# Layer norm by packed variances on column and row tiles, tap sums moved into the first blur, last blur rows added by VectorE

## The chip, the cores and the metric

One NeuronCore of a Trainium2 chip. The metric is the device time of one execution in microseconds (us), as the median of several runs. The kernel before takes 470.53 us (median of 3 runs, 469.13 to 471.44).

## What is computed

The input x has 8 images of 16 channels of 64 x 64 pixels in float32. Four layers follow each other:

- L0: a layer norm over the 16 channels at every pixel, three depthwise convolutions along the rows and three along the columns, a projection, and attention along rows and columns with 8 heads.
- L1 and L3: a blur with 9 x 9 weights that depend on the pixel, added to x, and then an instance norm over the 4096 pixels of each of the 128 planes.
- L2: 3 x 3 convolutions with binarised weights, batch norm, a residual and a clip.

The part of the reference around the change, cut to what matters:

```
# L0, at each pixel of an image
mean, var over the 16 channels;  x = (x - mean) / sqrt(var + 1e-5) * ln_w + ln_b
# L1, L3
enhanced = x + low_freq                      # low_freq: the blurred x
out = (enhanced - mean) / sqrt(var + 1e-5)   # over the 4096 pixels of a plane
# L2: out1 = conv(x + shift1, sign(w)), out2 = conv(x + shift2, sign(w)), out = out1 + w1 * out2
```

## The kernel before, in words

The 128 partitions hold 8 images times 16 channels, and the free axis the 4096 pixels, in 8 chunks of 512 (one bank of PSUM, the tile `ps`, each). Each layer is one or more blocks; a block gives every engine its own list of instructions, semaphores order them by hand, and the next block begins when all engines have ended their lists. There are only a few loops in the program (the middle heads of the attention); all else is written out.

**`l0_norm` (L145 to L359)** is the first block. SyncE's queue loads `centre` and x in four parts (L201), then stores the summed taps to DRAM (`band`, L204), waits for that and loads them back shifted (`windows`, L212), then loads the tables that later layers need (L214). ScalarE's queue loads nine small constants (L299, L302) and ScalarE waits for all of them (L303). TensorE multiplies each chunk by `centre` (x minus its mean, L240), VectorE copies the result to `xc` (L336), ScalarE squares it (L306). Variances come from eight matmuls with `meansel` (L251), each on a tile of 32 columns of the array, into two banks; they are copied out (L340, L309), turned by transposes (L259), get eps added (L345), then a square root (L311) and a reciprocal over 256 elements (L348). The 256 values per partition are widened to 4096 by eight copies on VectorE and eight on ScalarE (`widen`, L294), and 32 transposes turn them back (L268). VectorE scales each chunk (L354), ScalarE applies weight and bias (L318), and TensorE turns the chunks into `xrow` and `xcol` (L282), which VectorE and ScalarE copy out in turns (L359, L324). GpSimd meanwhile clears `pad_a` and builds `toep` with two large products (L224, L228) from `windows`. The next block, `l0_conv`, begins with matmuls on `toep` (L430).

**`blur` (L882 to L1267)** runs twice, for L1 (tag g1) and L3 (tag g3), over 8 rows of blocks r. TensorE computes logits on row tiles (L1065), ScalarE takes exp (L1074), TensorE sums (L1088) on column tiles, VectorE swings, normalises and turns the sums (L1098, L1106, L1113), and GpSimd adds them to the padded image (`pool_enhance`, L1118); VectorE takes statistics of that row (`dve_stats`, L1123). After the last row come the mean, the variance and `norm` (L1254 to L1259). In the first blur VectorE also makes the binary weights `wb` (L1273, L1275).

**`binconv` (L1279 to L1446)** normalises 8 groups of 8 rows (VectorE, L1370), rounds them to `high` (ScalarE, L1362), takes `rest` as the difference (VectorE, L1375), and convolves both parts with nine taps, 18 matmuls per group (TensorE, L1346). Behind the first group TensorE computes the tap sums, nine matmuls with two columns (L1354), into bank 7; VectorE waits for them (L1398), makes a map of them (to L1424), and then goes through the groups (L1425 on).

Of the kernel before, what the change touches and what calls it, by code (L numbers as in the profile page):

```python
# [23 lines left out]
F32 = mybir.dt.float32  # L24
# [38 lines left out]
        "g1_b1", "g1_b2", "g3_b1", "g3_b2"]  # L63
# [8 lines left out]
def build(nc, d, band, out):  # L72

    keep = ExitStack()
    with keep:
# [50 lines left out]
        with ExitStack() as g:  # L126
            negative = sb(g, "negative", [P, TAPS * P])
            raw, raw_in = later["c_weight"]
            wb_ready = sem("wb_ready")
            blur(nc, sem, lambda n, s: sb(g, "g1_" + n, s), "g1", later, ident, vec, ps, pad_a, norm, pad_b, None, None,  # L130
                 beside=lambda dve: binary_weights(dve, raw, negative, wb, raw_in, wb_ready))
        with ExitStack() as c:
            binconv(nc, sem, lambda n, s: sb(c, n, s),
                    lambda n, s: c.enter_context(nc.sbuf_tensor(n, s, F32R)), vec, ps, wb, norm, pad_a, pad_b)
# [10 lines left out]
def l0_norm(nc, sem, sb, d, ident, vec, pad_a, ps, x0, xrow, xcol, toep, onehot, beta,  # L145
            projblk, const_in, later, band, x_again):


    centre = sb("centre", [P, P])
    meansel = sb("meansel", [P, 32])  # L150
    var_row = sb("var_row", [P, 2 * BANK])
# [8 lines left out]
    var = sb("var", [P, PXT * B])  # L160
    std = sb("std", [P, PXT * B])
    rstd = sb("rstd", [P, PXT, B])
    wide = sb("wide", [P, PXT, CP, B, HEADS])

    x_in = [sem(f"x_in{j}") for j in range(4)]
    centre_in = sem("centre_in")
    centred = sem("centred")
# [11 lines left out]
    var_out = [sem(f"var_out{a}") for a in range(2)]  # L179
    var_turned = sem("var_turned")  # L180
    eps_added = sem("eps_added")
    rooted = sem("rooted")
    rstd_ready = sem("rstd_ready")
    rstd_wide = [sem(f"rstd_wide{cp}") for cp in range(CP)]
# [6 lines left out]
    CONSTS = 8  # L191

    with nc.Block() as block:
        @block.sync
        def _(sp):
# [38 lines left out]
        def _(pe):  # L234
            pe.wait_ge(centre_in, 16)

            for j in range(CHUNKS):
# [4 lines left out]
            pe.wait_ge(const_in, 16 * CONSTS)  # L242
            pe.wait_ge(xc_copied, 5)

            pe.matmul(ps[:, 4, 0:2], bias_rhs[:], bias_lhs[:], start=True, stop=True).then_inc(bias_mm, 1)

            for a in range(2):
                pe.wait_ge(xc_copied, 6 + a)
                for q in range(4):
                    pe.wait_ge(squared, 4 * a + q + 1)  # L250
                    mm = pe.matmul(ps[32 * q:32 * q + 32, 5 + a, :], meansel[:],  # L251
                                   sq[:, BANK * (4 * a + q):BANK * (4 * a + q + 1)], start=True, stop=True)
                mm.then_inc(var_mm, 1)

            for a in range(2):
                pe.wait_ge(xc_copied, 1 + a)
                pe.wait_ge(var_out[a], 1)
                for c in range(4):
                    tr = pe.transpose(ps[:, a, P * c:P * c + P], var_row[:, BANK * a + P * c:BANK * a + P * c + P],  # L259
                                      ident[:])  # L260
                tr.then_inc(var_turned, 1)

            pe.wait_ge(bias_read, 1)
            for t in range(PXT):
                if t % 4 == 0:
                    for cp in range(CP):
                        pe.wait_ge(rstd_wide[cp], t // 4 + 1)
                tr = pe.transpose(ps[:, t // 4, P * (t % 4):P * (t % 4) + P],  # L268
                                  wide[:, t].rearrange("p c b n -> p (c b n)"), ident[:])
                if t % 4 == 3:  # L270
                    tr.then_inc(rstd_spread, 1)

            for base, lines in ((0, sq[:].rearrange("p (i m) -> p i m", m=P)),
# [17 lines left out]
        def widen(copy, j, cp):  # L291

            tiles = slice(4 * j, 4 * j + 4)
            copy(wide[:, tiles, cp], spread(rstd[:, tiles, :].unsqueeze(3), [P, 4, B, HEADS]))\  # L294
                .then_inc(rstd_wide[cp], 1)

        @block.scalar
        def _(act):
            act.dma_start(taps[:], d["taps"]).then_inc(taps_in, 16)  # L299
            for t, name in ((meansel, "meansel"), (ident, "ident"), (vec, "vec"), (bias_lhs, "bias_lhs"),  # L300
                            (bias_rhs, "bias_rhs"), (onehot, "onehot"), (mask, "mask"), (projblk, "projblk")):
                act.dma_start(t[:], d[name]).then_inc(const_in, 16)  # L302
            act.wait_ge(const_in, 16 * CONSTS)  # L303
            for j in range(CHUNKS):
# [3 lines left out]
            act.wait_ge(var_mm, 2)  # L308
            act.copy(var_row[:, BANK:2 * BANK], ps[:, 6, :]).then_inc(var_out[1], 1)  # L309
            act.wait_ge(eps_added, 2)  # L310
            act.activation(std[:], var[:], ACT.Sqrt).then_inc(rooted, 1)  # L311
            act.wait_ge(rstd_ready, 1)
            for j in range(CHUNKS):
                widen(act.copy, j, 1)

            for j in range(CHUNKS):
# [1235 lines left out]
```

## Time and profile before

| | |
|---|---|
| median of 3 runs | 470.53 us |
| the profiled execution | 471.36 us |
| span of its trace, first to last instruction | 469.4 us |
| TensorE matmuls busy | 394.1 us (84%) |
| VectorE busy | 276.3 us (59%) |
| ScalarE busy | 241.5 us (51%) |
| GpSimd busy | 108.2 us (23%) |

In the rows below PE is TensorE (PEld its weight loads), DVE VectorE, ACT ScalarE, POOL GpSimd, SP SyncE; L336 is line 336 of the kernel before. A float32 matmul stands as two records (passes) in the trace; a transpose or an fp32r matmul as one. Times of the timeline are microseconds from the start of the span; spans on POOL are rough.

### The profile page before, as it was taken

The page shows a single profiled execution, that of the slowest core. Times are in us where ns is not written, and L with a number is a line of the kernel's source. Part 1 is how long each engine was busy: PE and PEld are TensorE (multiplying, and loading weights), DVE is VectorE, ACT ScalarE, POOL GpSimd, SP SyncE. Part 2 cuts the span into 40 slices and gives each one's busy share as a digit, 9 for nine tenths or more (in the row PEclk, how much of TensorE's full clock was granted, in tenths as well). Part 3 has the DMA queues.
Part 4 walks back from the last instruction along what each step waited for, and adds up shares of the span by engine and source line. Part 5 has one row for each costly group of instructions (what it writes and reads, how often), then busy time and mean ns, then how long its engine had stood idle before and what let it go on. Part 6 is the DMA issues. An engine that isn't in the chain of part 4 may idle for free. (4 is left out here: it accounts for less than half of the span.)

```text
span 469.4 us, 15959 instructions
## 1 busy us (share of the span) xinstructions
PE 394.1 (84%) x7136; PEld 245.7 (52%) x7136; DVE 276.3 (59%) x459; ACT 241.5 (51%) x310; POOL 108.2 (23%) x134
## 2 busy tenths in 40 slices
PE   4758998887499999988899999939998889999980
PEld 1247882322289885134555555528773555555550
DVE  1697369576378889747744353465845654343453
ACT  1548258566543331143478888810103538888772
POOL 3050002122200000075027223110007513224211
PEclk9959999898999999989999999969999999999995
DMA  8860000000000000000000000000000000000004
GB/s 182 166 257 1 1 1 1 0 1 0 1 3 3 1 3 1 1 1 1 1 4 4 4 3 5 4 1 0 1 0 2 1 1 4 4 4 3 4 4 179
DMA packets 8239, 10.14 MB, mean 22 GB/s; under 512 B 5535, under 2 KB 6896, under 8 KB 8048
## 3 DMA queue, kind: packets, MB, share of 16 engines
q1 hardware_dynamic: 7152, 8.82, 6.8%
q8 instruction: 54, 0.88, 0.8%
q10 hardware_dynamic: 1024, 0.36, 0.4%
q14 instruction: 9, 0.07, 0.1%
HBM read 7.06 MB, written 2.11 MB: 20 GB/s over the span
## 5 line engine op out<-in xcount | busy, mean ns | idle before, releaser
L1074 ACT ACTIVATE g_wgt<-ps 128x1024 f32<-128x1024 f32 x128 | 124.1, 1021 | 39.6 <-PE ps L1065 39.6
L1088 PEld LDWEIGHTS ps<-g_wgt,g_xt 128*17 128x17 f32 x4096 | 58.8, 97 | 47.7 <-ACT g_wgt L1074 43.1
L1065 PE MATMUL ps<-g_diag,g_exponents 32*128 32x512 f32 x512 | 73.7, 638 | 9.0 <-ACT g_wgt L1074 5.2
L1088 PE MATMUL ps<-g_wgt,g_xt 128*17 128x64 f32 x4096 | 69.9, 220 | 2.6 <-DVE g_xt L1051 1.9
L1098 DVE STREAM_TRANSPOSE g_swung<-ps 128x512 f32<-128x512 f32 x32 | 23.0, 717 | 80.1 <-PE ps L1088 80.1
L1130 POOL TENSOR_TENSOR g_diag<-g_scl,hot 128x512 f32<-128x512 f32 x32 | 33.3, 1059 | 32.1 <-PE ps L1065 25.4
L1346 PE MATMUL ps<-high,wb 128*128 128x512 f32 x72 | 30.4, 423 | 8.1 <-DVE rest L1375 8.1
L470 PE MATMUL ps<-conv_img,projblk 128*32 128x512 f32 x256 | 35.5, 689 | 0.0
L527 ACT ACTIVATE biased<-ps,beta_o 128x512 f32<-128x512 f32 x32 | 24.7, 799 | 15.7 <-PE ps L470 15.7
L1065 PEld LDWEIGHTS ps<-g_diag,g_exponents 32*128 32x128 f32 x512 | 21.4, 182 | 19.2 <-ACT g_wgt L1074 8.1
L1346 PE MATMUL ps<-rest,wb 128*128 128x512 f32 x72 | 30.1, 418 | 0.0
L974 ACT ACTIVATE g_hid<-ps,vec 128x512 f32<-128x512 f32 x16 | 11.0, 688 | 33.8 <-PE ps L961 33.8
L667 ACT ACTIVATE e<-ps 128x512 f32<-128x512 f32 x16 | 9.6, 597 | 31.7 <-PE ps L629 31.7
L1051 DVE COPY g_xt<-ps 128x512 f32<-128x512 f32 x30 | 19.5, 683 | 8.8 <-PE ps L1045 8.8
L470 PEld LDWEIGHTS ps<-conv_img,projblk 128*32 128x32 f32 x256 | 13.0, 118 | 21.6 <-issue 17.5
L1045 PE MATMUL ps<-ident,g_wgt 128*128 128x128 f32 x144 | 20.5, 281 | 4.4 <-DVE g_xt L1051 3.8
L1118 POOL TENSOR_TENSOR pad_b<-pad_b,g_low 128x512 f32<-128x512 f32 x8 | 10.2, 1269 | 51.2 <-DVE g_low L1113 51.2
L1045 PEld LDWEIGHTS ps<-ident,g_wgt 128*128 128x128 f32 x144 | 15.2, 140 | 12.4 <-issue 8.8
L1029 POOL COPY g_wgt<-pad_b 128x512 f32<-128x512 f32 x18 | 10.3, 626 | 46.6 <-POOLq L1335 45.0
L1118 POOL TENSOR_TENSOR pad_a<-pad_a,g_low 128x512 f32<-128x512 f32 x8 | 10.1, 1269 | 46.5 <-DVE g_low L1113 46.5
L1346 PEld LDWEIGHTS ps<-high,wb 128*128 128x128 f32 x72 | 14.5, 202 | 12.1 <-DVE rest L1375 8.3
L618 PE MATMUL ps<-ident,rnh 128*128 128x128 f32 x128 | 18.8, 295 | 2.3 <-POOL rnh L710 2.3
(164 smaller groups left out, 640.0 us busy)
## 6 DMA issues: line engine op xcount, KB each, us to landing
x<-in_x SPq DMA_DIRECT2D x8, 256.0 KB, 7.0
x<-in_x SPq DMA_DIRECT2D x1, 2048.0 KB, 8.7
out<-pad_a SPq DMA_DIRECT2D x4, 512.0 KB, 3.9
windows<-band SPq DMA_DIRECT2D x4, 256.0 KB, 5.1
c_weight<-in_c_weight SPq DMA_DIRECT2D x1, 576.0 KB, 4.3
g_gband<-in_g_gband SPq DMA_DIRECT2D x2, 128.0 KB, 2.9
g_w<-in_g_w SPq DMA_DIRECT2D x2, 128.0 KB, 2.7
onehot<-in_onehot ACTq DMA_DIRECT2D x1, 128.0 KB
```

The lines of the kernel that those rows point to most:

```text
L470: mm = pe.matmul(ps[q:q + 32, j % 4, :], projblk[:, 64 * cp + 32 * late:64 * cp + 32 * late + 32], lines(t, inner, strip, side), start=Tru ...
L527: act.activation(biased[:, j % 4, :], ps[:, j % 4, :], ACT.Identity, bias=beta[:, t:t + 1], scale=1.0).then_inc(proj_biased, 1)
L618: tr = pe.transpose(ps[:, NORM[t % 2], P * k:P * k + P], spread(rnh[s][:, 4 * t + k:4 * t + k + 1], [P, P]), ident[:])
L1045: tr = pe.transpose(ps[:, XT_BANK[k], P * j:P * j + P], tile(g)[:, cb].rearrange("p r c -> p (r c)"), ident[:])
L1051: copy(xt[g][:, 4 * k:4 * k + 4, :, 0:C], ps[:, XT_BANK[k], :].rearrange("p (k b m) -> p k b m", k=4, b=B)).then_inc(done, 1)
L1065: mm = pe.matmul(ps[:, pair(2 * f + g // 2) + g % 2, :], gband[part, t, :], diag[r % 2][h][part].rearrange("p a n -> p (a n)"), start=True ...
L1074: act.activation(wgt[r % 2][h][:, t, parity].rearrange("p u a n -> p (u a n)"), ps[:, pair(n):pair(n) + 2, :].rearrange("p u n -> p (u n)" ...
L1088: mm = pe.matmul(ps[32 * j:32 * j + MX, O_BANK[h], 64 * cb:64 * cb + 64], xt[r + t][:, cb, 2 * j + h, :], wgt[r % 2][h][:, t, parity, :, 4 ...
L1098: dve.transpose(swung[h][:].rearrange("p a n -> p (a n)"), ps[:, O_BANK[h], :]).then_inc(swung_out, 1)
L1118: pool.tensor_tensor(rows, rows, low[r % 2][:].rearrange("p (k r c) -> p r k c", k=CB, r=BLK), ALU.add)\
L1130: pool.tensor_tensor(diag[r % 2][h][:], spread(own.unsqueeze(2), [P, 16, 32]), spread(hot[:].unsqueeze(1), [P, 16, 32]), ALU.mult).then_in ...
L1346: mm = pe.matmul(ps[:, g % 4, :], wb[:, t, :], part[:, ROWS * g + dh:ROWS * g + dh + ROWS, dw:dw + W], start=(k == 0), stop=(k == 2 * TAPS ...
```

## The change

It has four parts. In `l0_norm`, the variances of four chunks are packed into one 128 x 128 piece by 16 matmuls with N = 128 on four column tiles, ScalarE takes the square root of it directly from PSUM (eps as its bias, after a first square root of one column that only brings the table), VectorE inverts it, and 16 matmuls on four row tiles spread it over the four chunks' banks; this is done for each half of the chunks, the first half ahead of the last two centring matmuls. The loads change places: ScalarE's queue loads the taps, `meansel` (now 64 KB) and `vec`, stores `band`, and loads three more; SyncE's queue takes `spreadsel` (new, 64 KB), `ident`, `onehot` and `projblk`, the last two behind `windows`. In the blurs, the last row is added by VectorE in place of GpSimd. The tap sums are computed at the end of TensorE's list in the first blur, into bank 4. And the first group of the convolutions takes its nine `high` taps as soon as `high` is there, and then the nine `rest` taps.

```diff
@@ l0_norm, @block.sync
-            sp.wait_ge(taps_summed, 2)
-            sp.dma_start(band, taps[:, 0, :]).then_inc(band_out, 16)
+            sp.dma_start(spreadsel[:], d["spreadsel"]).then_inc(spreadsel_in, 16)
+            sp.dma_start(ident[:], d["ident"]).then_inc(tables_in, 16)
             sp.wait_ge(band_out, 16)
...
+            for t, name in ((onehot, "onehot"), (projblk, "projblk")):
+                sp.dma_start(t[:], d[name]).then_inc(tables_in, 16)
             for name, (t, arrived) in later.items():
@@ l0_norm, @block.tensor
+            def variances(a):
+                pe.wait_ge(xc_copied, PART * (a + 1))
+                pe.wait_ge(squared, PART * (a + 1))
+                for v in range(PART):
+                    for u in range(PART):
+                        first = BANK * (PART * a + u) + P * v
+                        mm = pe.matmul(ps[32 * u:32 * u + 32, PART * a, 0:P], meansel[:, v, :],
+                                       sq[:, first:first + P], start=(v == 0), stop=(v == PART - 1))
+                mm.then_inc(var_mm, 1)
+            def spread_out(a):
+                pe.wait_ge(rstd_ready, a + 1)
+                for v in range(PART):
+                    for u in range(PART):
+                        part = slice(32 * u, 32 * u + 32)
+                        mm = pe.matmul(ps[:, PART * a + u, P * v:P * v + P], spreadsel[part, v, :],
+                                       rstd[part, a, :], start=True, stop=True)
+                mm.then_inc(rstd_spread, 1)
+            for j in range(6):
+                centre_of(j)
+            pe.wait_ge(first_in, 16 * FIRST)
+            variances(0)
+            for j in range(6, CHUNKS):
+                centre_of(j)
...
+            pe.wait_ge(spreadsel_in, 16)
+            spread_out(0)
+            variances(1)
+            pe.wait_ge(bias_read, 1)
+            spread_out(1)
+            pe.wait_ge(tables_in, 16 * TABLES)
@@ l0_norm, @block.scalar
+            for t, name in ((meansel, "meansel"), (vec, "vec")):
+                act.dma_start(t[:], d[name]).then_inc(first_in, 16)
+            act.wait_ge(taps_summed, 2)
+            act.dma_start(band, taps[:, 0, :]).then_inc(band_out, 16)
+            for t, name in ((bias_lhs, "bias_lhs"), (bias_rhs, "bias_rhs"), (mask, "mask")):
                 act.dma_start(t[:], d[name]).then_inc(const_in, 16)
+            act.wait_ge(first_in, 16 * FIRST)
+            act.activation(root_first[:], vec[:, VEC["ln_eps"]:VEC["ln_eps"] + 1], ACT.Sqrt)
+            for j in range(6):
+                square(j)
+            root(0)
+            for j in range(6, CHUNKS):
+                square(j)
+            root(1)
@@ l0_norm, @block.vector
+            for j in range(6):
+                copy_out(j)
+            inverse(0)
+            for j in range(6, CHUNKS):
+                copy_out(j)
...
+            for j in range(2):
+                scale(j)
+            inverse(1)
+            for j in range(2, CHUNKS):
+                scale(j)
@@ blur
-                pool_enhance(pool, r)
+                if r + 1 < RB:
+                    enhance(pool, r)
...
+            if after_sums is not None:
+                after_sums(pe)
...
+            enhance(dve, RB - 1)
             dve_stats(dve, RB - 1)
+TAP_BANK = 4
+def tap_sums(pe, ps, wb, vec, ready, done):
+    pe.wait_ge(ready, 2)
+    for t in range(TAPS):
+        mm = pe.matmul(ps[:, TAP_BANK, 2 * t:2 * t + 2], wb[:, t, :].bitcast(F32), ...)
+    mm.then_inc(done, 1)
@@ binconv, @block.tensor
+            pe.wait_ge(rounded, 1)
+            for t in range(TAPS):
+                tap(0, t, high, t == 0, False)
+            pe.wait_ge(split, 1)
+            for t in range(TAPS):
+                mm = tap(0, t, rest, False, t == TAPS - 1)
...
-                if g == 0:
-                    for t in range(TAPS):
-                        mm = pe.matmul(ps[:, TAP_BANK, 2 * t:2 * t + 2], wb[:, t, :].bitcast(F32), ...)
-                    mm.then_inc(tap_mm, 1)
```

## Rows read from the trace of the kernel before

**Rows 1.** Timeline of the first 46 us: start, length (us), engine, line, [idle before <-releaser].

```profile
14.05 4.26 ACT L306 ACTIVATE sq<-xc 128x512 f32<-128x512 f32 x8 [3.05 <-DMA projblk<-in_projblk]
14.42 0.69 DVE L336 COPY xc<-ps 128x512 f32<-128x512 f32 x1 [0.17 <-PE ps L240]
...
14.75 1.98 PE L240 MATMUL ps<-x,centre 128*128 128x512 f32 x4 [0.37 <-DMA x<-in_x]
...
21.80 1.75 DVE L348 RECIPROCAL rstd<-std 128x256 f32<-128x256 f32 x1 [0.66 <-ACT std L311]
...
22.86 3.60 POOL L224 TENSOR_TENSOR toep<-windows,mask 128x2048 f32<-128x2048 f32 x1 [17.71 <-DMA windows<-band]
...
23.59 7.84 DVE L294 COPY wide<-rstd 128x256 f32<-128x256 f32 x8
...
26.42 3.65 POOL L228 TENSOR_TENSOR toep<-windows,mask 128x2048 f32<-128x2048 f32 x1
...
31.35 2.47 DVE L354 TENSOR_TENSOR xc<-xc,ps 128x512 f32<-128x512 f32 x4
32.06 5.76 ACT L318 ACTIVATE sq<-xc,vec 128x512 f32<-128x512 f32 x8 [5.93 <-DVE xc L354]
...
45.13 8.83 PE L430 MATMUL ps<-xrow,toep 128*128 128x256 f32 x32 [2.19 <-PEq L193]
```

**Rows 2.** Line L294 alone: durations in ns, minimum/median/maximum, first and last start.

```profile
L294 DVE COPY wide<-rstd x8: 279/280/3683, 23.6 to 31.1; 128x256 f32<-128x256 f32 x8
```

**Rows 3.** Groups by line: busy us, mean ns of one, idle before.

```profile
L1435 DVE TENSOR_TENSOR resid<-pad_a,shift_map 128x512 f32<-128x512 f32 x8 | 5.5, 685 | 0.0
...
L558 DVE RECIPROCAL rn<-root 128x128 f32<-128x128 f32 x1 | 1.0, 953 | 0.4 <-ACT root L535 0.4
...
L535 ACT ACTIVATE root<-nsq 128x128 f32<-128x128 f32 x1 | 0.3, 309 | 3.4 <-DVE nsq L556 3.4
```

**Rows 4.** Timeline of TensorE in three later stretches, columns as in rows 1.

```profile
298.06 1.14 PE L1065 MATMUL ps<-g_diag,g_exponents 32*128 32x512 f32 x8 [0.22 <-ACT g_wgt L1074]
299.13 1.09 PE L1088 MATMUL ps<-g_wgt,g_xt 128*17 128x64 f32 x64
...
319.85 2.06 PE L1354 MATMUL ps<-vec,wb 128*128 128x2 f32 x18
321.78 0.49 PE L1346 MATMUL ps<-high,wb 128*128 128x512 f32 x1
...
356.00 0.65 PE L990 MATMUL ps<-g_hid,g_w 128*32 128x128 f32 x16 [0.18 <-DVE g_hid L981]
```

**Rows 5.** Timeline from the first blur's last row to the first convolution.

```profile
306.59 0.71 DVE L1113 STREAM_TRANSPOSE g_low<-g_mix 128x512 f32<-128x512 f32 x1
307.38 1.26 POOL L1118 TENSOR_TENSOR pad_a<-pad_a,g_low 128x512 f32<-128x512 f32 x1 [5.91 <-DVE g_low L1113]
308.67 0.69 DVE L1123 BATCH_NORM_STATS2 g_stats<-pad_a 128x6 f32<-128x512 f32 x1 [1.37 <-POOL pad_a L1118]
...
312.27 0.85 DVE L1375 TENSOR_TENSOR rest<-pad_a,high 128x660 fp32r<-128x660 f32 x1 [0.38 <-ACT high L1362]
...
313.18 0.79 PE L1346 MATMUL ps<-high,wb 128*128 128x512 f32 x1 [8.14 <-DVE rest L1375]
```

**Rows 6.** Line L1118, both blurs: who waited for it (us in total, times).

```profile
  DVE g_stats L1123: 2.7, 2
```

**Rows 7.** Stretches: length, busy us (instructions) of PE, PEld, DVE, ACT, POOL; granted clock; DMA.

```profile
46.00:48.00 2.00, 2.00 (x6) 1.64 (x5) 0.69 (x1) 0.00 (x0) 0.00 (x0) 0.50 0.01 4
49.00:52.00 3.00, 3.00 (x15) 2.64 (x15) 1.28 (x2) 0.94 (x2) 0.00 (x0) 1.00 0.00 0
...
313.20:318.00 4.80, 4.80 (x11) 3.77 (x12) 1.61 (x7) 0.65 (x1) 0.00 (x0) 0.50 0.00 0
...
322.00:340.00 18.00, 18.00 (x77) 14.20 (x77) 16.26 (x42) 3.28 (x5) 0.00 (x0) 1.00 0.00 1
```

**Rows 8.** DMA issues: KB each, us to landing.

```profile
band<-taps SPq DMA_DIRECT2D x1, 15.9 KB, 8.7
```

More of the change, by code:

```diff
@@ L234, in _, with centre_of @@
         def _(pe):
-            pe.wait_ge(centre_in, 16)
-            for j in range(CHUNKS):
+            def centre_of(j):
                 if j % 2 == 0:
@@ L299, in _, with square @@
             act.dma_start(taps[:], d["taps"]).then_inc(taps_in, 16)
-            for t, name in ((meansel, "meansel"), (ident, "ident"), (vec, "vec"), (bias_lhs, "bias_lhs"),
-                            (bias_rhs, "bias_rhs"), (onehot, "onehot"), (mask, "mask"), (projblk, "projblk")):
+            for t, name in ((meansel, "meansel"), (vec, "vec")):
[3 more added lines that the diff above has]
+            for t, name in ((bias_lhs, "bias_lhs"), (bias_rhs, "bias_rhs"), (mask, "mask")):
                 act.dma_start(t[:], d[name]).then_inc(const_in, 16)
-            act.wait_ge(const_in, 16 * CONSTS)
-            for j in range(CHUNKS):
+            def square(j):
                 act.wait_ge(xc_copied, j + 1)
@@ L307, in _, with root @@
                                ACT.Square).then_inc(squared, 1)
[L308 to L314, printed above, removed]
+            def root(a):
+                act.wait_ge(var_mm, a + 1)
+                act.activation(std[:, a], ps[:, PART * a, 0:P], ACT.Sqrt,
+                               bias=vec[:, VEC["ln_eps"]:VEC["ln_eps"] + 1], scale=1.0).then_inc(rooted, 1)
+            act.wait_ge(first_in, 16 * FIRST)
[6 more added lines that the diff above has]
+            root(1)
             for j in range(CHUNKS):
@@ L879, in l0_out, with blur @@
     return on_tensor, on_scalar, on_vector
-def blur(nc, sem_, sb, tag, later, ident, vec, ps, pad, norm, to_clear, result, out, beside=None):
+def blur(nc, sem_, sb, tag, later, ident, vec, ps, pad, norm, to_clear, result, out, beside=None, after_sums=None):
     def sem(name):
@@ L1337, in _, with tap @@
         def _(pe):
-            for g in range(CHUNKS):
+            def tap(g, t, part, first, last):
+                dh, dw = t // 3, t % 3
+                return pe.matmul(ps[:, g % 4, :], wb[:, t, :],
+                                 part[:, ROWS * g + dh:ROWS * g + dh + ROWS, dw:dw + W], start=first, stop=last)
+            pe.wait_ge(rounded, 1)
[4 more added lines that the diff above has]
+                mm = tap(0, t, rest, False, t == TAPS - 1)
+            mm.then_inc(conv_mm, 1)
+            for g in range(1, CHUNKS):
                 pe.wait_ge(split, g + 1)
@@ L1341, in _ @@
                     pe.wait_ge(lin_ready, g - 3)
[L1342 removed]
                 for t in range(TAPS):
[L1344 to L1356 removed]
+                    tap(g, t, high, t == 0, False)
+                    mm = tap(g, t, rest, False, t == TAPS - 1)
+                mm.then_inc(conv_mm, 1)
         @block.scalar
@@ L1473, in shape_constants @@
     onehot = np.tile(np.eye(8, 32, dtype=np.float32), (P, 1, 1))
-    return {"ident": ident, "centre": centre, "meansel": meansel,
+    return {"ident": ident, "centre": centre, "meansel": meansel, "spreadsel": spreadsel,
             "onehot": onehot, "mask": mask, "gmask": gmask, "hot": hot}, (u, v, inside)
```

112 lines of the change are left out of this document (37 added, 75 removed).

## The prediction

> **What bounds the kernel now.** I read the timeline first, stage by stage, because a share over the whole span says nothing of the three places that change. In each place the question is which wait ends last.
>
> *Layer norm.* The block runs one chain [rows 1]. ScalarE's squares don't begin until 14.05: they wait for `projblk`, the last of nine constants, though VectorE is by then about to copy chunk 5 (14.42 + 0.69 = 15.11). The inverse root is there at 23.55 (21.80 + 1.75). Then comes the dearest piece: eight widening copies hold VectorE for 7.84 us, to 31.43. They are not long of themselves. The shortest and the median take 0.28 us, the longest 3.68 [rows 2]; in 23.59 to 30.1 GpSimd runs its two `toep` products of 3.60 and 3.65 us [rows 1], and the longest copy is about as long as one of them. Scaling follows (pitch 2.47 / 4 = 0.62 us), then weight and bias on ScalarE (pitch 5.76 / 8 = 0.72), which end at 37.82, and the turning up to the next block's first matmul at 45.13.
>
> *End of each blur.* VectorE's turned row is ready at 307.30; GpSimd adds it, and VectorE's statistics begin at 308.67 after an idle 1.37 us [rows 5]. It occurs twice, 2.7 us in all [rows 6].
>
> *Convolutions.* TensorE starts at 313.18 because `rest` ends at 313.12 (312.27 + 0.85); `high` was there at 312.27 [rows 5]. From then TensorE sets the end: in 322 to 340 it is busy 18.00 of 18 us, VectorE 16.26 [rows 7]. Between groups 0 and 1 the tap sums take 319.85 to 321.78 [rows 4].
>
> **The change, part by part.** Prices are for one execution; the sum is made against the profiled one, 471.36 us.
>
> *1. Norm: the new schedule, in times of the trace before.* Arrival of x and the centring of chunks 0 to 5 stay. Squares now wait for two constants, not nine, so the square of chunk 5 follows its copy (15.11) at a pitch of 0.53 (4.26 / 8 [rows 1]) plus start-up: 15.8. The 16 variance matmuls are 32 passes with 32 columns and N = 128; the like in the blur is 16 passes in 0.65 us [rows 4], so 1.3 us, 14.3 to 15.6, before this half's last square ends and so free. They do push centring of chunks 6 and 7 (1.98 us [rows 1]) to 17.6. Root: 0.31, inverse: 0.95 (both from the 128 x 128 rows [rows 3]): 17.1. Copies of chunks 6 and 7 stand behind that inverse on VectorE: 2 x 0.69, 18.5; the square of 7: 19.1.
>
> Spreading is not in the trace with N = 128. Below: one logit fill moves as many columns through four row tiles, 1.14 us [rows 4]. Above: 32 passes one after another, each at the tap sums' pitch, 2.06 / 18 = 0.114: 3.65 us. I take 1.5, near the fill, since the tiles are the same; four sets of weights instead of one are the addition. First spread 17.95 (behind the bias matmul) to 19.45, second variances to 20.75, root to 21.1, inverse to 22.05 (VectorE scales chunks 0 and 1 meanwhile), second spread to 23.6, scaling of 4 to 7 to 26.1, weight and bias to 26.9. Before that was 37.82. The turning behind it is unchanged, so the next block begins **10.9 us** earlier, at 34.2. By the bounds of spreading, two spreads at 1.14 give 0.7 more, at 3.65 they give 4.3 less.
>
> *2. Its loads.* ScalarE now waits for the tap sums on VectorE before it stores `band`; behind that wait stand three small loads and then the squares. It costs nothing as long as ScalarE is through before chunk 0's copy; it issues five loads fewer ahead of the squares than before, and the new first root's table load is also taken there. If the two constants came as late as the nine did (14.05), the chain would lose 1.5. `band` stood behind x on SyncE's queue and took 8.7 us [rows 8]; if it lands no earlier, the windows, and `toep` with its end at 30.1 [rows 1], stay as they were, still 4 us ahead of 34.2. `onehot` and `projblk` stand behind `windows` now; turning needs them, but VectorE and ScalarE empty the banks only from 26.1 on, so that is the cover. `spreadsel` and `ident` go ahead of the windows, two issues on SyncE; the later layers' tables are needed long after. All at nothing.
>
> *3. Last row on VectorE.* In place of 1.37 us idle stands one addition with two inputs in SBUF; the row of `resid` has 0.685 [rows 3], and it can begin where GpSimd's began, at 307.38. Statistics begin near 308.07: **0.60**, twice: **1.20**. GpSimd has nothing else at that time.
>
> *4. First group.* It starts when `high` is there, 312.27 in place of 313.18: **0.91**. `rest` is then ready long before nine matmuls have passed.
>
> *5. Tap sums.* They leave TensorE between groups 0 and 1: **1.93** (321.78 - 319.85 [rows 4]). In the blur they follow its last sums, where TensorE idles 8.14 us [rows 5]; that cover is four times their 2.06. VectorE has its map earlier and would wait for TensorE, not the other way round.
>
> Sum: 10.9 + 1.20 + 0.91 + 1.93 = 14.94. 471.36 - 14.94 = **456.4**. The profiled execution stands 0.83 above the median of 470.53, within the runs shown; from the median it would be 455.6. I give **456.0**.
>
> *The clock.* TensorE's granted clock is 0.50 (1.2 GHz) when the convolutions start after the idle 8.14 us, and 11 matmuls take 4.80 us (0.44 each) against 77 in 18.00 (0.23) at full level [rows 7]; group 0 thus takes 6.67 us (313.18 to 319.85), against 18 x 0.23 = 4.2: 2.5 us lost. The same occurs at the start of the block after the norm: 6 passes in 2 us at 0.50, 15 in 3 at 1.00 [rows 7]. Its idle time before stays about 2.2 us there, and shrinks from 8.14 to some 4.6 at the convolutions (tap sums until 307.1, start at 311.7). I take no difference; between none lost at both places (-4.2) and half as much again (+2).
>
> *Two rules weighed.* A copy that waited for GpSimd's whole product is in rows 2. The Trainium skill (SBUF — State Buffer, "SBUF: two separate sides") says why: a VectorE operation in a two-port mode, or with two SBUF inputs against a GpSimd operation that reads SBUF, and a GpSimd operation lock each other out for a whole instruction. By that rule the new second inverse could wait, which is rival C; copies and scalings from PSUM would not. Second, fills on row tiles and sums on column tiles alternate, and the sums start at 299.13 while the fill ends at 299.20 [rows 4]: no gap. The Trainium skill (TensorEngine Tiling (Array Packing), "Tiling Modes") says that changing the tiling mode drains TensorE. The norm would change mode six times; by the rule, at one pass of the tap sums' pitch each (0.114, an estimate), the sum would be near 457.1; the trace speaks against it.
>
> **The rivals.**
>
> *A, the forecast:* 456.0; 453.5 to 458.5 with the clock's moods. 0.60.
>
> *B, tiles one after another:* the spreads cost 3.65 each, the next block starts 4.3 later: 456.4 + 4.3 = 460.7. For it: so short a pass on row tiles is not in the trace. Against: the fill's overlap. 0.13.
>
> *C, the second inverse is held by `toep`:* it is issued near 21.1, when GpSimd may be in its products, and would wait until one or both end. At most a whole product, 3.65, and up to 456.4 + 3.65 = 460.1. Against: before, `toep` began at 22.86 while the inverse of 1.75 us was running, and both ran on [rows 1]. 0.08. The rule of the page on SBUF in the Trainium skill, told above, is the one that would do this.
>
> *D, full clock:* the tap sums shorten TensorE's idle time enough that the convolutions start at full level: 2.5 more off, 453.9; with the block behind the norm 452.2. For it: 4.6 us idle instead of 8.14. Against: 2.2 us was enough at 45.13. 0.13.
>
> *E, the change does not do what it says:* the squares still start at 14.05 or the tables come behind 26: 1.5 to 2 less off, 458. 0.03.
>
> *F, slower:* the place is the 64 small matmuls on tiles of the norm, 128 passes, of which my schedule gives 2 x 1.3 + 2 x 1.5 = 5.6 us. If every pass had to empty the array before the next, it would decide from (14.94 + 5.6) / 128 = 0.16 us a pass; at twice the tap sums' pitch, 0.23, the norm would take 128 x 0.23 = 29.4 us there, 23.8 more than planned, and the kernel 456.4 + 23.8 = 480.2. Against: 16 passes in 0.65 us, 0.04 each [rows 4]. 0.03.
>
> **How the numbers follow.** The likeliest case gives 456.0. For 8 in 10 the range takes A, D's own time and B: 452.0 to 461.0, which leaves out F, some of D and of C. About 0.5% (2.35 us) is what a measurement of this kernel can tell from no change; A to E all gain more than that, but for an unforeseen stall I keep 0.03 for slower and 0.02 for the same: faster 0.95.
>
> **What would show it.** In the profile after: squares at the pace of VectorE's copies, well before 14.05; no L294 group; weight and bias ending near 27, the first matmul on `toep` near 34 (B: near 38.5; C: a long reciprocal). One table load in the norm, not two. Statistics of the last row directly behind VectorE's own addition, twice. Tap sums right behind the blur's last sums, `high` matmuls from about 1.5 us earlier relative to the blur's end, and no gap between groups 0 and 1. A next block that still begins after 40, or any of the two spreads above 3.65 us, would prove the main step wrong.

## The result, and the profile after

The kernel after takes **455.35 us** (median of 4 runs, 452.71 to 457.71) against 470.89 (469.13 to 471.44, 4 runs) for the kernel before beside it: a ratio of 0.9677, 95% interval 0.9639 to 0.9715. The forecast was 456.0 and faster, in a range of 452.0 to 461.0. The profiled execution took 456.62 us, 14.74 less than the 471.36 of before; the sum of the prediction was 14.94.

The span and the engines' totals stand at the head of the page of the kernel after (share of the span, instructions):

```profile
span 454.6 us, 16078 instructions
...
PE 389.5 (86%) x7208; PEld 241.0 (53%) x7208; DVE 270.1 (59%) x451; ACT 240.9 (53%) x302; POOL 105.7 (23%) x132
```

They say little; the stages do. First the timeline of the norm, with the columns of [rows 1], which it answers:

```profile
5.25 1.28 ACT L324 ACT_TABLE_LOAD   x1 [5.25 <-issue]
...
8.36 7.94 SPq L215 DMA_DIRECT2D windows<-band  x4
...
9.39 0.63 ACT L314 ACTIVATE sq<-xc 128x512 f32<-128x512 f32 x1 [2.65 <-DVE xc L352]
...
14.03 1.08 PE L253 MATMUL ps<-sq,meansel 128*32 128x128 f32 x32
...
15.04 1.98 PE L243 MATMUL ps<-x,centre 128*128 128x512 f32 x4
...
17.26 1.17 PE L262 MATMUL ps<-rstd,spreadsel 32*128 32x128 f32 x32
...
20.22 0.95 DVE L356 RECIPROCAL rstd<-std 128x128 f32<-128x128 f32 x1 [0.43 <-ACT std L319]
...
20.73 3.60 POOL L229 TENSOR_TENSOR toep<-windows,mask 128x2048 f32<-128x2048 f32 x1 [15.59 <-DMA windows<-band]
...
21.32 1.17 PE L262 MATMUL ps<-rstd,spreadsel 32*128 32x128 f32 x32 [1.56 <-DVE rstd L356]
...
21.75 4.45 ACT L333 ACTIVATE sq<-xc,vec 128x512 f32<-128x512 f32 x6 [0.16 <-DVE xc L360]
...
22.42 8.18 PE L293 MATMUL ps<-ident,sq 128*128 128x128 f32 x64
22.55 2.48 DVE L360 TENSOR_TENSOR xc<-xc,ps 128x512 f32<-128x512 f32 x4 [0.24 <-PE ps L262]
...
24.29 3.60 POOL L233 TENSOR_TENSOR toep<-windows,mask 128x2048 f32<-128x2048 f32 x1
...
33.53 0.67 PE L449 MATMUL ps<-xrow,toep 128*128 128x256 f32 x2 [2.93 <-PEq L198]
```

To be seen: the groups of 32 passes take 1.08 and 1.17 us. The second inverse (20.22) runs its 0.95 us although the first `toep` product starts beside it at 20.73. VectorE scales at its old pitch (2.48 / 4 = 0.62) under that product. Weight and bias end at 26.20 (21.75 + 4.45), 37.82 before, and the next block starts at 33.53 in place of 45.13: 11.6 us earlier.

Then the end of the first blur, up to the convolutions, which answers [rows 5]:

```profile
294.74 1.61 PE L1310 MATMUL ps<-vec,wb 128*128 128x2 f32 x13
...
296.38 0.71 DVE L1132 STREAM_TRANSPOSE g_low<-g_mix 128x512 f32<-128x512 f32 x1
...
296.54 0.72 PE L1310 MATMUL ps<-vec,wb 128*128 128x2 f32 x5 [0.18 <-issue]
297.12 0.69 DVE L1138 TENSOR_TENSOR pad_a<-pad_a,g_low 128x512 f32<-128x512 f32 x1
297.85 0.69 DVE L1143 BATCH_NORM_STATS2 g_stats<-pad_a 128x6 f32<-128x512 f32 x1
...
301.45 0.84 DVE L1410 TENSOR_TENSOR rest<-pad_a,high 128x660 fp32r<-128x660 f32 x1 [0.38 <-ACT high L1397]
301.48 3.72 PE L1374 MATMUL ps<-high,wb 128*128 128x512 f32 x9 [4.22 <-ACT high L1397]
```

From the transpose of the last row to the statistics it is 1.47 us (297.85 - 296.38), before 2.08 [rows 5]: 0.61 saved. The wait for GpSimd [rows 6] is gone. The convolutions begin at 301.48, when `rest` has only just been started (301.45). The tap sums are through at 297.26, before the statistics. From the transpose to the convolutions it is 5.10 us in place of 6.59.

Last the stretches of the kernel after that answer [rows 7] (length, busy time of PE, PEld, DVE, ACT, POOL, granted clock, DMA):

```profile
34.80:38.00 3.20, 3.20 (x9) 2.51 (x8) 0.73 (x2) 0.58 (x1) 0.00 (x0) 0.50 0.00 0
...
301.50:304.40 2.90, 2.90 (x7) 2.32 (x8) 2.76 (x10) 1.23 (x3) 0.00 (x0) 0.50 0.00 0
...
117.00:123.40 6.40, 6.01 (x58) 5.21 (x60) 2.75 (x4) 2.62 (x4) 0.67 (x7) 0.50 0.01 3
```

Both blocks are still at 0.50 (1.2 GHz) at or just behind their start. The last line lies between the projection and the attention, where the change touches nothing, and is 0.50 too. Among the stretches at 0.50 in the trace of before are three of 3.4 us each from 110.1, 127.2 and 202.3. The last of them lies at the start of the first blur, where the trace of after has none: from the blur's first matmul to its first logits it is 20.20 us before (201.78 to 221.98) and 18.81 after (193.36 to 212.17).

Where the time went, as the lead of the kernel after at milestones of the two traces:

| milestone | before | after | lead |
|---|---|---|---|
| first matmul on `toep` | 45.13 | 33.53 | 11.60 |
| last projection matmul | 117.48 | 105.91 | 11.57 |
| attention begins | 127.35 | 117.39 | 9.96 |
| its output begins | 179.41 | 170.71 | 8.70 |
| first logits of the first blur | 221.98 | 212.17 | 9.81 |
| last row turned (VectorE) | 306.59 | 296.38 | 10.21 |
| statistics of the last row | 308.67 | 297.85 | 10.82 |
| convolutions begin | 313.18 | 301.48 | 11.70 |
| convolutions end | 352.06 | 337.40 | 14.66 |
| last row of the second blur | 457.64 | 443.46 | 14.18 |
| its statistics | 459.73 | 444.94 | 14.79 |
| end of span | 469.37 | 454.59 | 14.78 |

The four parts are seen in their places: 11.60, 0.61, 0.88, 2.96 (the tap sums and a shorter stretch at 0.50) and 0.61. Between them, in blocks that the change doesn't touch, 2.9 us are lost up to the attention's output, 1.5 won back up to the first blur's last row, most of it at that blur's start, and 0.5 lost in the second blur.

### The profile page after: what moved, and what is told of

Read it like the earlier page. It is cut to its first block and busy times, and to the rows that moved or that the text cites. A ratio compares the mean times of both kernels' runs of the same rounds, so it can differ in the third digit from the quotient of the medians.

```text
span 454.6 us, 16078 instructions
## 1 busy us (share of the span) xinstructions
PE 389.5 (86%) x7208; PEld 241.0 (53%) x7208; DVE 270.1 (59%) x451; ACT 240.9 (53%) x302; POOL 105.7 (23%) x132
## 5 line engine op out<-in xcount | busy, mean ns | idle before, releaser
L489 PE MATMUL ps<-conv_img,projblk 128*32 128x512 f32 x256 | 37.5, 721 | 0.0
L546 ACT ACTIVATE biased<-ps,beta_o 128x512 f32<-128x512 f32 x32 | 26.3, 856 | 13.7 <-PE ps L489 13.7
L1374 PE MATMUL ps<-high,wb 128*128 128x512 f32 x72 | 28.9, 423 | 4.2 <-ACT high L1397 4.2
L1374 PE MATMUL ps<-rest,wb 128*128 128x512 f32 x72 | 27.6, 401 | 0.0
L1048 POOL COPY g_wgt<-pad_a 128x512 f32<-128x512 f32 x18 | 10.3, 620 | 41.8 <-SPq L1157 40.2
L1138 POOL TENSOR_TENSOR pad_b<-pad_b,g_low 128x512 f32<-128x512 f32 x7 | 8.9, 1268 | 45.0 <-DVE g_low L1132 45.0
L472 PE MATMUL ps<-sqs,onehot 128*32 128x512 f32 x64 | 9.9, 703 | 11.0 <-ACT sqs L536 11.0
```

Source lines behind the costliest of these rows:

```text
L489: mm = pe.matmul(ps[q:q + 32, j % 4, :], projblk[:, 64 * cp + 32 * late:64 * cp + 32 * late + 32], lines(t, inner, strip, side), start=Tru ...
L546: act.activation(biased[:, j % 4, :], ps[:, j % 4, :], ACT.Identity, bias=beta[:, t:t + 1], scale=1.0).then_inc(proj_biased, 1)
L1048: pool.tensor_copy(tile(g).rearrange("p (k o) r c -> p o k r c", o=2)[:, odd], cols.rearrange("p r (k c) -> p k r c", c=QC)).then_inc(stag ...
L1374: return pe.matmul(ps[:, g % 4, :], wb[:, t, :], part[:, ROWS * g + dh:ROWS * g + dh + ROWS, dw:dw + W], start=first, stop=last)
```

## The experiments

Most experiments start from the kernel after, two from the kernel before. The theories are those that each expectation names.

**Which part of the norm's gain is the collision with GpSimd?** In the kernel before, GpSimd's products wait until VectorE has made its widening copies; nothing else changes:

```diff
@@ l0_norm, @block.gpsimd
+            pool.wait_ge(rstd_wide[0], CHUNKS)
```

> The kernel before with one more wait: GpSimd begins its two toep products only when VectorE's eight widening copies are done. Theory 1 (two of the copies stood still because GpSimd's products held what they need): all eight copies take near 0.28 us, the group L294 on VectorE some 2.3 us instead of 7.84 and ends near 26; weight and bias end near 31 to 33 instead of 37.8, the next block begins near 38.5 to 40 instead of 45.1, the kernel takes 464 to 466. Theory 2 (the copies are slow of themselves, by their broadcast pattern): the group stays near 7.8 us, toep ends near 39, the next block still begins near 45, and the kernel takes 469.5 to 472.

Measured: 465.41 us (8 runs, 463.57 to 469.70), ratio 0.9912 (0.9873 to 0.9951). First the widening line of this kernel on VectorE (ns, minimum, median, maximum, first and last start), which answers [rows 2], then its timeline:

```profile
L295 DVE COPY wide<-rstd x8: 282/284/294, 23.6 to 25.0; 128x256 f32<-128x256 f32 x8
```

```profile
25.48 3.60 POOL L225 TENSOR_TENSOR toep<-windows,mask 128x2048 f32<-128x2048 f32 x1 [20.33 <-DVE wide L295]
26.04 6.11 ACT L319 ACTIVATE sq<-xc,vec 128x512 f32<-128x512 f32 x8
...
39.48 0.89 PE L431 MATMUL ps<-xrow,toep 128*128 128x256 f32 x3 [2.90 <-PEq L193]
```

No copy is long any more, weight and bias end at 32.15 and the next block begins at 39.48, 5.65 earlier than in [rows 1]. So 5.65 of the 11.60 us were not the old way of widening but its collision with the products: one wait in the kernel before gets them, as Theory 1 had it. The other half needs the new schedule; no run parts it further into the pieces of that schedule.

**Were the late constants worth anything?** In the kernel before, ScalarE waits for its constants behind the squares instead of ahead of them:

```diff
@@ l0_norm, @block.scalar
-            act.wait_ge(const_in, 16 * CONSTS)
...
+            act.wait_ge(const_in, 16 * CONSTS)
```

> The kernel before with ScalarE's wait for the nine constants moved behind its squares. Theory 1 (the last chunk's copy, which ends at 17.46, bounds the squares, whatever the constants do): the first square starts before 11 instead of at 14.05, the last one ends near 18.1 instead of 18.3, the next block begins within 0.5 of 45.1; the kernel takes 469 to 472. Theory 2 (the late constants are a term of the norm's gain, as the prediction's reading of the rows suggests): the chain behind the squares comes 2 to 3 us earlier, the next block near 42.5, the kernel near 468.

One run, 474.57 us. Two lines of its timeline:

```profile
9.50 0.63 ACT L305 ACTIVATE sq<-xc 128x512 f32<-128x512 f32 x1 [3.15 <-DVE xc L336]
...
44.66 1.64 PE L430 MATMUL ps<-xrow,toep 128*128 128x256 f32 x4 [2.05 <-PEq L193]
```

The first square comes 4.55 us earlier, the next block 0.47, of which x's earlier arrival in this run is 0.18. The squares catch up with VectorE's copies anyway, and the last of them, not the first, sets the chain. The block's start moves as Theory 1 had it. The whole is longer than its 469 to 472, but that is lost later: 2.8 us up to the first logits of the first blur, where one stretch at 0.50, from 120.2, lasts 13.7 us, and 0.9 in that blur.

**The norm alone.** From the kernel after, the other parts undone: GpSimd adds the last row again, the tap sums stand behind group 0, and group 0 waits for `rest`.

```diff
@@ the call of the first blur
-                 after_sums=lambda pe: tap_sums(pe, ps, wb, vec, wb_ready, tap_mm))
+                 after_sums=None)
@@ blur
-                if r + 1 < RB:
-                    enhance(pool, r)
+                enhance(pool, r)
...
-            enhance(dve, RB - 1)
@@ binconv, @block.tensor
-            pe.wait_ge(rounded, 1)
+            pe.wait_ge(split, 1)
             for t in range(TAPS):
                 tap(0, t, high, t == 0, False)
-            pe.wait_ge(split, 1)
-            for t in range(TAPS):
                 mm = tap(0, t, rest, False, t == TAPS - 1)
             mm.then_inc(conv_mm, 1)
+            for t in range(TAPS):
+                mm = pe.matmul(ps[:, TAP_BANK, 2 * t:2 * t + 2], wb[:, t, :].bitcast(F32), ...)
+            mm.then_inc(tap_mm, 1)
```

> The changed kernel with the blurs and the convolutions as they were before (GpSimd adds the last rows, the tap sums stand behind the first group, that group waits for rest): the layer norm's part alone. Theory 1 (the parts add up): the next block begins near 33.5, and the kernel takes 470.9 - 11.6 = 459.3, between 457.5 and 461. Theory 2 (the stages behind the norm give part of it back, whatever follows): 462 or more, with the loss between the first matmul on toep and the first blur.

Measured: 460.89 us (4 runs, 458.77 to 462.76), ratio 0.9806 (0.9750 to 0.9862). Its timeline at the end of the first blur:

```profile
298.10 1.26 POOL L1138 TENSOR_TENSOR pad_a<-pad_a,g_low 128x512 f32<-128x512 f32 x1 [5.51 <-DVE g_low L1132]
299.39 0.69 DVE L1143 BATCH_NORM_STATS2 g_stats<-pad_a 128x6 f32<-128x512 f32 x1 [1.37 <-POOL pad_a L1138]
...
303.89 0.80 PE L1372 MATMUL ps<-high,wb 128*128 128x512 f32 x1 [8.15 <-DVE rest L1410]
```

The idle 1.37 and 8.15 us of [rows 5] are back. Step by step against the kernel after it loses 0.61 at each blur, 0.88 at the start of the convolutions and 1.95 at their end: 4.05 us, where the prediction had 1.20 + 0.91 + 1.93 = 4.04. 460.89 lies in Theory 1's range of 457.5 to 461. The medians differ by 5.2 to 5.5 us (two sets of runs of the kernel after); the 1.2 to 1.5 beyond 4.05 are less than the spread of either kernel's runs, some 4 to 5 us.

**Does the order of the tiles matter?** From the kernel after, both loops of the variances and of the spreading are swapped, so that one tile does its four passes before the next:

```diff
@@ l0_norm, variances and spread_out
-                for v in range(PART):
-                    for u in range(PART):
+                for u in range(PART):
+                    for v in range(PART):
```

> The changed kernel with the two small loops of the norm turned round: all four matmuls of one tile follow each other, then the next tile's, the same 64 matmuls in all. Theory 1 (passes on different tiles run beside each other, passes on one tile can't; the forecast's price of 1.5 against rival B's 3.65): each group of 32 passes grows from 1.08 to 1.17 us to between 2.5 and 3.7, the next block begins at 37 to 41 instead of 33.5, the kernel takes 459 to 463. Theory 2 (32 short passes take the same in any order, their issue sets the time): each group stays between 1.0 and 1.4 us, the next block begins within 0.5 of 33.5, and the kernel takes 453 to 458.

One run, 465.87 us. TensorE's timeline, and two stretches with their granted clock (columns as above):

```profile
14.28 2.46 PE L253 MATMUL ps<-sq,meansel 128*32 128x128 f32 x32
...
18.90 2.82 PE L262 MATMUL ps<-rstd,spreadsel 32*128 32x128 f32 x32
21.64 4.05 PE L253 MATMUL ps<-sq,meansel 128*32 128x128 f32 x32
27.23 3.99 PE L262 MATMUL ps<-rstd,spreadsel 32*128 32x128 f32 x32 [1.53 <-DVE rstd L356]
...
42.28 0.89 PE L449 MATMUL ps<-xrow,toep 128*128 128x256 f32 x3 [1.80 <-PEq L198]
```

```profile
18.90:21.60 2.70, 2.70 (x33) 2.62 (x32) 0.55 (x2) 1.07 (x2) 1.24 (x1) 1.00 1.02 261
21.70:25.00 3.30, 3.30 (x29) 2.81 (x29) 1.28 (x2) 0.00 (x0) 3.30 (x2) 0.50 0.63 128
```

At the full level a group takes 2.46 and 2.82 us instead of 1.08 and 1.17, 0.08 to 0.09 a pass, and where the level fell to 0.50 it takes 4. The next block is 8.75 us later than after, more than expected, and the level fell in the middle of the norm, which is part of it. Rival B was a real danger; the order that alternates the tiles is what avoids it here. The kernel before, run once beside this and the next two, took 464.88 us, less than any other of its runs; these three are therefore read by their traces, not by their times.

**Is an inverse held by GpSimd's product, and a copy?** From the kernel after, one more operation of VectorE behind the scaling of chunk 3, where the first product runs; what it writes is not read by anything. The second kernel has the copy in place of the inverse:

```diff
@@ l0_norm
+    aside = sb("aside", [P, P])
@@ l0_norm, @block.vector
                 scale(j)
+                if j == 3:
+                    dve.reciprocal(aside[:], std[:, 0])
```

```diff
+                    dve.tensor_copy(aside[:], std[:, 0])
```

> The changed kernel with one more inverse on VectorE (128 x 128, from one SBUF tile into another that nobody reads), behind the scaling of chunk 3, when GpSimd is in its first toep product. Theory 1 (an inverse does not need what GpSimd's product holds): it takes 0.95 us and the next block begins 0.5 to 1.0 later than 33.5. Theory 2 (rival C's lock holds for an inverse too): it stands until that product ends, near 24.3, or the second, near 27.9, so 2 to 5.5 us long, and the next block begins 1.5 to 5.5 later.

> As the run before, with a plain copy (128 x 128, SBUF to SBUF) in place of the inverse. Theory 1 (a copy of this kind waits for GpSimd's whole product, as two of the widening copies did): it stands until a product ends, near 24.3 or 27.9, so 1.8 to 5.5 us long, though it has a quarter of a microsecond of work, and the next block begins 1.3 to 5 later than 33.5. Theory 2 (the widening copies waited for another reason): it takes under 0.4 us and the next block begins within 0.3 of 33.5.

The inverse (454.54 us), then the copy (456.55 us), each with the product beside it in its own timeline:

```profile
19.85 0.95 DVE L357 RECIPROCAL rstd<-std 128x128 f32<-128x128 f32 x1 [0.42 <-ACT std L320]
...
20.01 3.60 POOL L230 TENSOR_TENSOR toep<-windows,mask 128x2048 f32<-128x2048 f32 x1 [14.87 <-DMA windows<-band]
...
21.85 0.95 DVE L377 RECIPROCAL aside<-std 128x128 f32<-128x128 f32 x1
```

```profile
20.22 3.60 POOL L230 TENSOR_TENSOR toep<-windows,mask 128x2048 f32<-128x2048 f32 x1 [15.07 <-DMA windows<-band]
...
20.73 0.95 DVE L357 RECIPROCAL rstd<-std 128x128 f32<-128x128 f32 x1 [0.43 <-ACT std L320]
...
22.74 1.16 DVE L377 COPY aside<-std 128x128 f32<-128x128 f32 x1
```

The inverse takes its 0.95 us in the midst of the product. The copy of as many elements has 1.16 us and ends at 23.90, when the product (20.22 + 3.60 = 23.82) has ended. The next block begins 0.10 and 1.23 later than after, but not all of this is theirs: x does not arrive at the same time in every trace, and the norm's own second inverse, ahead of both, starts 0.37 earlier in the first kernel (19.85) and 0.51 later in the second (20.73) than after (20.22). So the inverse put the block back by 0.47 and the copy by 0.72. A copy of twice the elements takes 0.28 undisturbed (the first experiment). So the copy waits for the product and the inverse doesn't: rival C falls. The wait was shorter than expected, because the copy came late in the product.

**Is the clock's share to be had?** TensorE gets matmuls that nothing reads in three gaps: three behind the turning in the norm, ten behind the tap sums, five ahead of the convolutions (the same line as the ten, at the head of TensorE's list in `binconv`).

```diff
@@ l0_norm, @block.tensor (end)
+            pe.wait_ge(evac_v, 5)
+            for _ in range(3):
+                pe.matmul(ps[:, 0, :], ident[:], sq[:, 0:BANK], start=True, stop=True)
@@ tap_sums (end)
+    for _ in range(10):
+        pe.matmul(ps[:, 5, :], wb[:, 0, :], wb[:, 0:4, :].rearrange("p t m -> p (t m)"), ...)
```

> The changed kernel with matmuls whose result nobody reads, in two idle stretches of TensorE: three behind the norm's last turning (then the next block), and ten behind the tap sums and five ahead of the first convolution. Theory 1 (TensorE's level falls because it idles there, and the filling keeps it up): no stretch at 0.50 over the first matmuls on toep nor over the first convolutions; the first block of matmuls on toep takes 1.5 to 1.8 us less, the convolutions 1.2 to 1.6 less, the kernel 2.5 to 3.5 us less than the changed kernel timed beside it. Theory 2 (the filling delays what follows, or the level falls all the same and later): less than 1 us in all, or a loss.

Measured: 454.30 us (6 runs, 451.27 to 456.22), ratio 0.9650 (0.9613 to 0.9687). Its stretches at the two places, and TensorE's timeline at the second:

```profile
34.70:38.00 3.30, 3.30 (x16) 2.91 (x17) 1.19 (x2) 0.58 (x1) 0.00 (x0) 1.00 0.00 0
296.20:299.50 3.30, 3.30 (x10) 2.63 (x10) 1.52 (x6) 0.20 (x1) 0.00 (x0) 0.50 0.00 0
```

```profile
296.31 4.04 PE L1317 MATMUL ps<-wb 128*128 128x512 f32 x10
300.65 1.38 PE L1383 MATMUL ps<-wb 128*128 128x512 f32 x5 [0.30 <-PEq L1160]
302.19 2.16 PE L1379 MATMUL ps<-high,wb 128*128 128x512 f32 x8
```

At the norm it works: the block on `toep` begins at 1.00 and is 1.69 us shorter. At the convolutions the level fell under the filling itself; the ten took 4.04 us, the convolutions began 2.24 late and were 1.32 shorter.

**More of it.** The next kernel adds two such matmuls ahead of the last sums of squares in the second block and two behind its last transposes, where the trace of after is at 0.50:

```diff
@@ l0_conv, @block.tensor (ahead of the last norm_sums, and at the end)
+            for _ in range(2):
+                pe.matmul(ps[:, 4, :], ident[:], toep[:, 0, 0:4, :].rearrange("p c w -> p (c w)"), ...)
```

> As the run before, with two more pairs of such matmuls at the end of the second block (ahead of its last sums of squares and behind its last transposes). The stretches at 0.50 between 100 and 125 us have come in lengths of 3.4 to 13.7 us from run to run. Theory 1 (idle TensorE there sets them): they are gone or at most 3.4 us, the step from the last projection to the end of the attention shrinks by 1 to 3 us, and the kernel takes 3.5 to 6 us less than the changed kernel beside it. Theory 2 (the filling stands ahead of the sums in TensorE's queue and only delays them): no more than the run before, or up to 2 us worse than it.

> The changed kernel itself, timed beside the two runs before. Every theory: within 1% of 455.35; the stages off TensorE's level take the same to 0.1 us as in its first trace, and the differences from trace to trace lie where the stretches at 0.50 fall.

On the same chip the filled kernel took 449.83 us (6 runs, 447.72 to 453.28), ratio 0.9579 (0.9540 to 0.9617), and the kernel after, again, 455.69 (5 runs, 453.17 to 457.22), ratio 0.9696 (0.9664 to 0.9727). So the first filling gains 1.39 us beside it, less than the 2.5 to 3.5 of its Theory 1, with intervals that overlap; this one gains 5.86, within the 3.5 to 6 of its Theory 1. The stretches of the filled kernel, then of this second trace of the kernel after:

```profile
33.30:36.70 3.40, 3.40 (x16) 3.01 (x17) 1.24 (x2) 0.59 (x1) 0.00 (x0) 1.00 0.00 0
109.00:124.00 15.00, 13.52 (x238) 11.00 (x239) 9.98 (x18) 6.08 (x11) 1.24 (x8) 1.00 0.01 2
296.70:300.00 3.30, 3.29 (x14) 2.63 (x15) 3.09 (x13) 1.28 (x3) 0.00 (x0) 1.00 0.00 0
```

```profile
22.70:26.00 3.30, 3.30 (x35) 3.08 (x28) 2.58 (x5) 2.82 (x4) 3.30 (x2) 0.50 0.83 253
34.80:38.00 3.20, 3.15 (x15) 2.82 (x16) 0.97 (x2) 0.59 (x1) 0.00 (x0) 1.00 0.00 0
109.00:124.00 15.00, 11.91 (x166) 8.66 (x160) 7.65 (x14) 4.95 (x8) 1.20 (x8) 0.81 0.00 1
```

Filled, all three places run at 1.00. Against the first trace of after the blocks are shorter by 1.69 (on `toep`), 1.47 (projection), 1.48 (norms of the heads), 2.21 (attention) and 1.30 (convolutions). The 1.47 are not shown to be the filling's: none stands in that stage, and the second trace of the kernel after is 2.84 shorter there. The gain at the end of the second block repeats: in all three traces with that filling (this one and the two below) the norms of the heads take 10.0 us and the attention 51.1, in the two of the kernel after 11.5 and 11.8, 53.3 and 52.1 (in the one of before 9.9 and 52.1).

The second trace of the same kernel after has its stretch at 0.50 in the norm, at 22.7, and the block on `toep` at 1.00: where the level falls moves from run to run. That block begins at 34.85 there, 1.32 later than in the first trace; 0.85 of it is x, with VectorE's first scaling at 19.35 for 18.50. The expected agreement to 0.1 us off the level does not hold throughout: the first blur, from first logits to last row, takes 84.57 us there and 84.21 in the first trace, both at 1.00.

Two more kernels part the places: the fillings of the norm and the second block without those around the convolutions, and the filled kernel a second time.

> The filling behind the norm and at the end of the second block alone; none behind the tap sums or ahead of the convolutions. Theory 1 (the filling at the convolutions is worth nothing on the mean: it saves some 1.3 us where the level holds, and starts the convolutions some 2 us late where the level falls under it): within 1 us of the version with all the filling, timed beside it. Theory 2 (it is worth its 1.3 us): 1 to 2 us slower than that version.

> The version with all the filling once more, beside the run before. Both theories: 0.955 to 0.962 of the kernel before, near 450 us.

Measured: 454.05 us (6 runs, 452.04 to 456.08), ratio 0.9632 (0.9592 to 0.9673), and 453.17 (6 runs, 451.28 to 455.17), ratio 0.9621 (0.9581 to 0.9662). The two can't be told apart, so the filling around the convolutions isn't shown to be worth anything; in the second trace of the filled kernel the level fell under it again, and the convolutions began 2.37 late. The filled kernel's second time is 3 us above the expected 450 and its ratio just outside 0.955 to 0.962. In its two measurements the filled kernel has ratios of 0.9579 and 0.9621, the kernel after 0.9677 and 0.9696. On one chip side by side their intervals lie apart; the second interval of the filled kernel overlaps the first of the kernel after, which did not run beside it. So it beats the kernel before both times, and the kernel after in the one comparison side by side; by the ratios it gains 2.6 to 5.5 us over the kernel after.

## Why the prediction was right

*The norm: 10.9 forecast, 11.60 measured.* The schedule held in its order and nearly in its times. Variances 1.08 us for 1.3, spreads 1.17 for 1.5, near the lower bound of 1.14: the fill on row tiles [rows 4] was the right row. The second spread ends at 22.49 (forecast 23.6), weight and bias at 26.20 (26.9); 0.4 of that first lead of 1.1 is lost again, because ScalarE, at a pitch of 4.45 / 6 = 0.74, and not VectorE's scaling sets the end. Of the 0.7 too little, 0.28 is x, whose first chunk is copied at 8.67 in place of 8.95; that it would come earlier I had not said. Whether the change does this isn't shown, since x's arrival moves from trace to trace. The second trace of the kernel after begins the next block at 34.85, a lead of 10.28, so a part of the close fit is luck. The root of the first half took 0.35, its inverse 0.95, for 0.31 and 0.95.

*What the reading of it weighed wrongly.* It began with the squares' wait for the constants and named the widening second. The experiments turn this round: the constants give 0.3 us alone, the collision 5.65. The mechanism of the collision was read off rightly from [rows 2], but how much of the gain it is stood nowhere, and with it that a single wait would have brought half. The Trainium skill (SBUF — State Buffer, "SBUF: two separate sides") gives the reason, an exclusive lock for a whole instruction. The copies agree with it (0.28 us with no product beside them in the first experiment, 1.16 beside one, 3.68 in [rows 2]), and the inverse is not held (0.95 us beside a product too).

*The loads: nothing, and nothing it was.* `windows` are issued from 8.36, and `toep` begins at 20.73 in place of 22.86, because `band` no longer stands behind x. It ends at 27.89 (24.29 + 3.60), well ahead of 33.53. `onehot`, `projblk` and the tables hold up nobody. The prediction's five loads fewer on ScalarE's queue are a miscount: three leave it and the store of `band` joins it. Nothing hangs on it, as ScalarE is through with its first root at 6.74, ahead of chunk 0's copy.

*Last rows: 0.60 each, measured 0.61 twice; `high` first: 0.91, measured 0.88.* The addition takes 0.69 us, as the row of `resid` said.

*Tap sums: 1.93, measured 1.95 by undoing them.* At their new place they last longer, 2.52 us with a gap (294.74 to 297.26, for 2.06), and are still through 4.2 us before the convolutions.

*The clock: no difference taken.* Both blocks did come to 0.50 once more, so rival D fell. The stretch at the convolutions was shorter, 2.9 us for 5.2, worth the 1.0 by which the lead there grew beyond the tap sums. The bounds gave the block behind the norm 1.7 without a row; the first filled kernel shows 1.69 there. The parts together gave 15.65 us (11.60 + 1.22 + 0.88 + 1.95) for the forecast 14.94, and the rest of the program gave 0.9 back: 1.0 at the convolutions and 1.5 up to the first blur's last row won, 2.9 and 0.5 lost. That these nearly cancel was luck: the zero between the bounds of -4.2 and +2 was a choice, and it looked for the level at two places only.

*The other rivals.* B and F needed passes of 0.114 and 0.23 us; measured were 1.08 / 32 = 0.034 and 1.17 / 32 = 0.037. The Trainium skill's rule that a change of the tiling mode drains TensorE (TensorEngine Tiling (Array Packing), "Tiling Modes") shows no cost here that the trace resolves: centring goes on at 15.04, while the variances' passes end at 15.11 (14.03 + 1.08), and the turning starts at 22.42, while the second spread ends at 22.49. Ends of matmuls are modelled, so a cost below 0.1 us is not excluded. E fell: one table load in the norm, at 5.25, and squares from 9.39.

## What to carry to other kernels

Before a chain of small operations is rewritten, look at what its longest single one overlaps with on another engine: a copy from SBUF to SBUF on VectorE beside a large GpSimd product can cost a whole product, and moving one wait may bring half the gain. Small matmuls on several tiles of the array are to be issued in turns, a different tile each time; tile by tile the same passes took more than twice as long here (2.46 and 2.82 us for 1.08 and 1.17). A wait that ends late is worth only what it takes from the last link of its chain, so follow the chain to its end before it is priced.

## What had not been expected

TensorE's level of 0.50 doesn't stay at the places where the forecast looked for it. Over the traces of one and the same kernel it appears in the norm, at the start of the block on `toep`, or at the end of the second block, for 3 to 7 us (13.7 in three traces of variants), and moves a block by 1.0 to 2.2 us. The filled kernel, with the level at 1.00 at those places, is 2.6 to 5.5 us shorter, so some part of the spread of 452.7 to 457.7 among the runs of the kernel after may come from this; only one of these runs has a trace, so it is not shown. Filling an idle TensorE has a price of its own: issued when the level had already fallen, the ten matmuls took 4.04 and 4.61 us instead of 2.58, and then stood in the way of the block that they were to help.

The arrival of x moves as well: in the traces of the kernel after and its variants the copy of chunk 5 ends anywhere from 14.14 to 15.86 us. The start of the next block in a single trace can be compared with another only after this is taken off.

Three things stay open. The first is why the kernel before once took 464.88 us. The second is why the first blur was 2.6 us longer in the first trace of the filled kernel (449.83 us). There the profile shows TensorE twice standing idle ahead of its sums in the blur, 0.93 and 1.11 us, with nothing that it waits for; the second reads:

```profile
289.85 0.23 PE L1114 MATMUL ps<-g_wgt,g_xt 128*17 128x64 f32 x1 [1.11 <-issue]
```

Four other traces have one such stop near that place, of 0.9 to 1.5 us; what causes it is not shown. The third is whether filling around the convolutions is worth anything on the mean.
